# A prefetch hint for the loop-closing branch, at the head of every pass, in an attention and FP4 feed-forward block

## What is computed

```python
mod = (silu(c) @ wmod).reshape(8, 6, 1, 256)          # sa, ca, ga, sb, cb, gb
h = layernorm(x) * (1 + ca) + sa
x = x + ga * attention(h)
h = layernorm(x) * (1 + cb) + sb
x = x + gb * ffn(h)
```

## The kernel before

| stage | engines | line of the loop | passes, samples | written out |
|---|---|---|---|---|
| project | SP, DVE, POOL, PE, ACT | L240, L323, L353, L410, L478 | 7 (0 to 6) | sample 7 behind |
| attend | SP, PE, DVE | L632, L798, L959 | 6 (1 to 6) | 0 ahead, 7 behind |
| attend | POOL, ACT | L671, L839 | 7 (1 to 7) | 0 ahead |
| feed | PE, ACT, POOL, DVE | L1210 (in `run`) | 7 (1 to 7) | 0 ahead, the drain behind |
| feed | SP | L1228 | 7 (1 to 7) | 0 ahead |

## Time and profile before

### The profile page before, as it was taken

How to read it: one execution, slowest core, us unless ns; L and a number is a source line. 1 busy time by engine, 2 the same in 40 slices (tenths; PEclk the granted TensorE clock), 3 DMA queues, 4 the chain that set the end, 5 groups by cost and what they waited for, 6 DMA issues and landing times. The chain is left out here.

```text
span 2775.7 us, 54634 instructions
## 1 busy us (share of the span) xinstructions
PE 2597.7 (94%) x15110; PEld 1209.7 (44%) x15110; DVE 2345.5 (85%) x4659; ACT 1601.3 (58%) x2988; POOL 970.2 (35%) x865
## 2 busy tenths in 40 slices
PE   5887679999999999999999999999978999999998
PEld 3333213343444444344344344443323566666665
DVE  5888698888888888888888888888756999999997
ACT  3666507777777777777777777777762222222221
POOL 3666522122122122122122122122231555555654
PEclk8767659999999999999999999999997999999999
DMA  4777864446455455455456455456201111111110
GB/s 152 246 247 255 265 129 73 71 74 99 62 85 87 63 82 82 71 78 86 70 78 86 72 80 86 69 79 94 39 11 38 37 41 40 40 40 42 40 32 18
DMA packets 207121, 238.56 MB, mean 86 GB/s; under 512 B 32256, under 2 KB 150784, under 8 KB 206720
## 3 DMA queue, kind: packets, MB, share of 16 engines
q1 hardware_dynamic: 194560, 218.56, 40.7%
q0 software_dynamic: 3072, 8.39, 1.2%
q10 hardware_dynamic: 9216, 8.39, 0.9%
HBM read 149.79 MB, written 83.89 MB: 84 GB/s over the span
## 5 line engine op out<-in xcount | busy, mean ns | idle before, releaser
L856 DVE CUSTOM_DVE_ANT_0 unread<-max_ps,toeplitz_sb 128x1024 bf16<-128x1024 f32 x1024 | 1219.2, 1219 | 230.5 <-PE max_ps L689 221.9
L817 ACT ACTIVATE probs<-score_ps 128x512 f32<-128x512 f32 x2048 | 1113.3, 597 | 438.3 <-PE score_ps L722 299.7
L689 PE MATMUL max_ps<-k_low,q_low 96*128 96x512 bf16 x2048 | 717.5, 393 | 30.0 <-DVE ident_bf L847 17.9
L651 POOL TENSOR_TENSOR probs<-probs,up_probs 128x512 f32<-128x512 f32 x256 | 336.8, 1316 | 624.4 <-ACT up_probs L821 624.4
L750 PE MATMUL pv_ps<-probs,v 128*32 128x512 f32 x4096 | 548.9, 608 | 3.4 <-POOL probs L651 3.4
L722 PE MATMUL score_ps<-q_low,k_low 99*128 99x512 bf16 (+3 forms) x1280 | 407.9, 320 | 4.9 <-ACT probs L817 4.1
L714 PE MATMUL score_ps<-q_up,k_up 99*128 99x512 bf16 (+3 forms) x1280 | 408.0, 319 | 4.5 <-ACT probs L817 3.8
L1284 PE MATMUL gu_ps<-wgu_t,turned 128*128 128x512 f32 (+1 forms) x768 | 314.7, 559 | 0.6 <-DVE hid L1445 0.6
L657 POOL DMA_DIRECT2D attn<-out_n x64 | 48.8, 762 | 698.3 <-DVE out_n L920 674.8
L714 PEld LDWEIGHTS score_ps<-q_up,k_up 99*128 99x128 bf16 x1280 | 123.8, 97 | 350.4 <-ACT probs L817 325.2
L689 PEld LDWEIGHTS max_ps<-k_low,q_low 96*128 96x128 bf16 x2048 | 194.0, 99 | 156.5 <-DVE row_max L856 83.9
(11 more groups left out here) (145 smaller groups left out, 3218.2 us busy)
## 6 DMA issues: line engine op xcount, KB each, us to landing
splits<-parts SPq DMA_DIRECT2D x128, 384.0 KB, 2.6
q_low<-splits SPq DMA_DIRECT2D x192, 128.0 KB, 4.4
k_low<-splits SPq DMA_DIRECT2D x192, 128.0 KB, 7.0
q_up<-splits SPq DMA_DIRECT2D x192, 128.0 KB, 9.4
k_up<-splits SPq DMA_DIRECT2D x192, 128.0 KB, 12.0
v_padded<-v_out SPq DMA_DIRECT2D x64, 256.0 KB, 3.5
v<-v_padded SPq DMA_DIRECT2D x32, 512.0 KB, 13.9
x_in<-in_L_attn_x SPq DMA_DIRECT2D x16, 512.0 KB, 4.6
```

What stands on the lines that cost most here:

```text
L651: nc.gpsimd.tensor_tensor(probs[:, g % PROBS, :, at:at + P], probs[:, g % PROBS, :, at:at + P], up_probs[:, g % 2], ALU.add).then_inc(diag ...
L689: mm = pe.matmul(max_ps[:, i % 2, half * HALF:(half + 1) * HALF], low[0][u][0:KROWS, h, qb * P:(qb + 1) * P], low[1][u][0:KROWS, h, half * ...
L817: nc.scalar.activation(probs[:, g % PROBS, h, :], score_ps[:, i % 2, :], ACT.Exp).then_inc(exp_done, 1)
L856: nc.vector.tensor_tensor_reduce(unread[:, i % 2, :], max_ps[:, i % 2, :], toeplitz[:, at:at + S], 1.0, -3.0e38, ALU.mult, ALU.max, row_ma ...
```

## The change

Each of the fifteen loops is opened through a helper that asks for a hint for the branch that closes the pass. The hint is one more instruction for the engine's sequencer, the first one of every pass. It names the compare-and-branch at the end of the pass, and says that it is likely taken. Bodies, counts of passes, semaphores and transfers are as before; `run` is handed the engine in place of its loop.

```diff
+def hinted(nc, eng, first, last):
+
+    return nc.Fori(first, last, engines=bass.OrderedEngineSet([eng.engine]), hint_back_edge=True)
...
-        with sp.Fori(0, B - 1) as b:
+        with hinted(nc, sp, 0, B - 1) as b:
...
-        with pe.Fori(1, B - 1) as b:
+        with hinted(nc, pe, 1, B - 1) as b:
             for u in range(UNITS):
                 unit_steps(b, u, False, False)
...
-    def run(loop, iteration):
+    def run(eng, iteration):
         for i in range(TILES):
             iteration(0, i)
-        with loop(1, B) as b:
+        with hinted(nc, eng, 1, B) as b:
             for i in range(TILES):
                 iteration(b, i)
...
-        run(pe.Fori, iteration)
+        run(pe, iteration)
```

More of the change, by code:

```diff
@@ L322, in _ @@
         statistics(0, 1)
-        with dve.Fori(0, B - 1) as b:
+        with hinted(nc, dve, 0, B - 1) as b:
             steps(b)
@@ L352, in _ @@
         inverse_std(1)
-        with pool.Fori(0, B - 1) as b:
+        with hinted(nc, pool, 0, B - 1) as b:
             low_parts(b, 0)
@@ L409, in _ @@
         turn(0, 0)
-        with pe.Fori(0, B - 1) as b:
+        with hinted(nc, pe, 0, B - 1) as b:
             steps(b)
@@ L477, in _ @@
         modulate(0, 0)
-        with act.Fori(0, B - 1) as b:
+        with hinted(nc, act, 0, B - 1) as b:
             steps(b)
@@ L631, in _ @@
             step(0, u, False)
-        with sp.Fori(1, B - 1) as b:
+        with hinted(nc, sp, 1, B - 1) as b:
             for u in range(UNITS):
@@ L670, in _ @@
             unit_steps(0, u, u == 0)
-        with pool.Fori(1, B) as b:
+        with hinted(nc, pool, 1, B) as b:
             for u in range(UNITS):
@@ L838, in _ @@
             unit_steps(0, u, u == 0)
-        with act.Fori(1, B) as b:
+        with hinted(nc, act, 1, B) as b:
             for u in range(UNITS):
@@ L958, in _ @@
             unit_steps(0, u, u == 0, False)
-        with dve.Fori(1, B - 1) as b:
+        with hinted(nc, dve, 1, B - 1) as b:
             for u in range(UNITS):
@@ L1227, in _ @@
             load(0, i)
-        with sp.Fori(1, B) as b:
+        with hinted(nc, sp, 1, B) as b:
             for i in range(TILES):
@@ L1349, in iteration @@
                 store(*tile_at(b, i, STORE))
-        run(act.Fori, iteration)
+        run(act, iteration)
         for i in range(2):
@@ L1396, in iteration @@
                 hidden_product(*tile_at(b, i, HIDDEN))
-        run(pool.Fori, iteration)
+        run(pool, iteration)
     @block.vector
@@ L1478, in iteration @@
                 residual_out(*tile_at(b, i, DOWN))
-        run(dve.Fori, iteration)
+        run(dve, iteration)
     st.close()
```

## The result

The changed kernel takes 2757.14 us in the median (2756.63 to 2762.02 over four runs), against 2778.11 us for the kernel before on the same chip: a ratio of 0.9927, 95% interval 0.9912 to 0.9941. It is faster, by 21.0 us, where 35.0 were forecast: inside the range, 13 us from the number. The profiled execution's span went from 2775.7 to 2755.5 us, with the mean granted clock at 0.941.

What follows compares the result with a forecast made beforehand. PE, busy 94% of the span, was taken as the bound, with DVE at 85%. Terms -37.2 + 0.9 + 1.3 = -35.0 us take span 2775.7 to 2740.7; adding 3.25 gives 2744.0 us, range 2739 to 2766.

Steps and rivals of the forecast that it cites:

- The size of what could be won: Hintable loss at loop edges: 26.7 us and 1.35 us in attention, 9.1 us in feed-forward, 37.2 us together.
- (2): DVE's feed-forward hint: stall falls from 2.8 to about 0.3 us, which costs nothing; gain 9.1 us.
- (1): Attention hints on PE, DVE and ACT: edges healed but for 0.15 us each, 0.9 us over six; bounds 0 and 1.8.
- rival A: The hint does nothing, since fetches during the pass might displace its target; 2780 us, chance 0.11.
- (5): Loop exits, where a hint saying taken is wrong at the last pass: taken as 0, bounds 0 and 9.7 us.
- (3): Hints on short passes (projection, SP, POOL, feed-forward PE and ACT): nothing was fetched there, so nothing is gained.
- (4): The hint instructions heading 20 passes in a row on each engine: cost 1.3 us, bounds 0 and 5.
- B: Rival: the hint heals some engines and not others; 2761 us if PE, 2770 if only the 8 KB queue; chance 0.10.
- C: Rival: slower, with new "issue" waits in the middle of a pass; 2787 us or above, chance 0.07.

Runs made afterwards that it cites:

- e6: e5 with ACT's attention code moved as a whole by an alignment, without a jump: 2742.78 us, ratio 0.986 to the kernel before.
- e3: The changed kernel with the hint on PE's attention loop alone: 2777.15 us, ratio 0.9989 to the kernel before.
- e7: The kernel before, without any hint, with e6's one alignment line for ACT's attention code: 2778.01 us in one run.
- e1: The changed kernel with ACT's attention loop placed, by a jump ahead of it, so its branch falls mid-block: 2756.68 us, ratio 0.9909 to the kernel before.
- e8: The changed kernel without the hint on DVE's projection loop, meant to shift DVE's later code by one instruction: 2759.68 us, ratio 0.9914 to the kernel before.
- e5: e2 with each hint's direction taken from a register, saying taken in all passes but the last: 2749.12 us, ratio 0.9886 to the kernel before.
- e2: The changed kernel with hints on four loops only (PE, DVE, ACT in attention, DVE in feed-forward): 2756.8 us, ratio 0.9918 to the kernel before.
- e4: e1 with DVE's attention loop moved too, its branch close behind a block's start: 2757.33 us, ratio 0.9918 to the kernel before.
- e9: e6 with its hints, taken in all passes but the last, on all fifteen loops: 2743.05 us, ratio 0.9863 to the kernel before.

## Why the prediction was right, and where it fell short

**The size of what could be won: right.** 37.2 us was read from marks, not from stalls. By the same marks e6 wins 26.8 us in the 20 units, 1.3 around the exit and 9.0 in the 48 tiles, 37.1 together; its median is 37.4 us below that of the kernel before. The reading that the three engines refill together held too: e3, with PE's stall gone, keeps 4.4 of 5.35 us for each edge. The clock's dips went with the stalls, as forecast, and are the smaller part of an edge's price: in e7 no dip follows the first three edges, and they still cost 5.0 to 5.5 us each.

**The feed-forward stage (2): right.** 9.0 us of 9.1.

**The attention edges (1): mis-sized.** The leftover was put at 0.15 us an edge, from the 0.3 us that ACT needs at a short loop's branch. That row was the wrong one to take, since there nothing is fetched. The 20 units kept 1023.7 - 1016.8 = 6.9 us, where 0.75 was forecast. Two things make it up. ACT's announced fetch comes late; moving its branch to mid-block takes away 4.5 us (e1). The rest, 2.4 us in e1, lies in the unit behind each edge unit (51.34 instead of 50.84), with DVE's wait of 0.4 us, which comes from where its sequencer's pause falls (e8). In place of its row the prediction needed one question: is the fetch finished when the branch comes? I had treated "the hint is a whole pass ahead" as a worry about displacement (rival A) and answered it with "the fetch can wait until the engine is near". That answer was right and was itself the danger: near can be too near.

**The exits (5): failed, by the value taken.** The mechanism was named and its bounds were 0 and 9.7 us, and I took 0, because the rest of the branch's block is there and the next fetch could run beside it. The runs show that it doesn't. The two units around the attention exit take 105.8 us, where 101.7 are two quiet ones, and 102.3 with the direction put right (e5). The wait there is PE's: 2.0 to 2.5 us before one and the same product, the one at 1850.84 us above, in all six kernels whose hint on PE is false at the exit (the change, e1, e2, e3, e4, e8), and in none of the other five. At the feed-forward exit DVE has 1.5 us of "issue" in the drain, which e5 doesn't have. By the marks the exits' right direction is worth about 4 us, under half of the upper bound. One reason was out of sight: the price isn't due at the branch, where I looked for it (PE's fall-through is 88 ns), but at the end of that block, 3 to 37 us later.

**The short loops (3) and the hint instructions (4).** Nothing gained there, as forecast. The 1.3 us for the instructions was too much: a hint takes 31 to 39 ns in most passes, and with hints on 15 loops or on 4 the time is the same (e9 against e6, e2 against the change).

So 35.0 us were forecast and 21.0 measured, 20.2 by the spans. Between 35.0 and 20.2 stand 6.2 us in the 20 units; 4.0 at the attention exit with ACT's lone edge; 3.0 of scatter at the start; and 2.9 in four small rows, less the 1.3 that the hints didn't cost. Of the small rows, 0.9 (fifth to ninth mark) and 0.6 (the nine tiles) are DVE's pause again: e2 has neither, with the same false hints at its exits. The 0.4 at the end goes with DVE's wait in the drain, and the 1.0 ahead of the feed-forward stage is within the scatter.

**The rivals.** A fell with PE's branch at 357 ns. The rule of the Trainium skill that it leaned on ("Runtime: NRT & Kernel Launch", section on instruction fetch mechanics), that prefetch is purely sequential, doesn't hold for a branch that a hint announces. What the same section says of a taken branch out of the window, that it forces a fetch, the trace agrees with where no hint stands: 3800 ns on PE and 3.4 and 3.5 us on DVE and ACT. The prediction used its window of two blocks against PE's 690 instructions, and left out that the section also gives PE room for 2048 instructions and the others room for 512. With those sizes PE's pass would fit, as the trace shows, and DVE's 380 instructions would fit too, which the trace contradicts with a stall of 2.8 us at each edge. B happened in a milder form: ACT half healed. Its price for PE alone, 2761 us, was wrong: e3 took 2777, since a stall of DVE and ACT together is not ACT's lone 1.35, and since the units at the exit, where PE's hint is false, took 4.1 us more. C was right in its mechanism, one fetch taking the place of another, and wrong in its place: at the exit, once for each loop, where the hint is false, and not in every pass.

## What to carry to other kernels

Before a hint is placed, find the loops whose branch really fetches: here four of fifteen, read from branch duration or from the gap to the next instruction. Then look at four things: whether the branch lies deep enough in its block that the announced fetch can finish (here 0.5 us of delay against 2 to 3), whether the hint is true at the last pass too, whether all engines that meet at the edge are healed, and whether a sequencer's pause now falls between a wait and the operation behind it (here 0.5 us a pass). Price an exit not at the branch but at the end of its block.

## What the runs showed of the hardware that was not expected

- An announced fetch seems to begin when the block with the branch is entered, not at the hint. The same hint leaves 0.4 us or 2.2 us on ACT, and 0.5 us or 3.0 us on DVE, by the branch's place alone (e1 and e4 against the change).
- A hint that is wrong at the exit delays code further on: a product on PE by 2.0 to 2.5 us, 2.6 us behind the branch, and an operation on DVE by 1.5 us, 22 us behind it in the feed-forward stage and 37 us behind it in attention (e2). A direction from a register works, and takes this away.
- DVE's sequencer pauses some 0.4 us about once in 128 instructions. Where the pause falls between a wait and its operation, the operation comes 0.4 us late (the change, e1, e8); one instruction later it costs nothing (e2, e5, e6).
- A healed branch on PE still takes 357 ns, against 208 ns at a short loop; ACT and DVE need 0.4 to 0.6 us to the next instruction. All of it is absorbed: units with such an edge take 50.84 us.
- An unannounced jump ahead of a loop costs 2.6 us on ACT (3.0 in e4), more than the 2.2 us of the edge it was meant to mend.
